# A four-layer transformer program on one core: the third layer with its routing inside the scan stage, and the first layer's row additions five in four heads

## The chip, the cores and the metric

One core of a Trainium2 chip runs the whole program in one launch. The metric is the device time of that launch in microseconds, on the core; lower is better. TensorE multiplies (its weight loads run beside its multiplications), VectorE, ScalarE and GpSimd compute on rows of 128 partitions, and SyncE issues most transfers. In the profile they are PE (and PEld), DVE, ACT, POOL and SP.

## What is computed

A tensor of 4 x 512 tokens of width 128 goes through four layers; each is an attention or state-space block beside a mixture of experts, both added to the running sum x. The stages that the change touches:

- Layer 0, attention: 16 heads of width 8 over each of four sequences, plain softmax. Its mixture of 64 experts has been computed before; each expert's 32 rows have yet to be added to their tokens' rows.
- Layer 2, both halves. From the normalized input xn (router weights, then two of eight experts each):

```python
logits = xf.astype(jnp.float32) @ w_router.T
gates = jax.nn.softmax(logits, axis=-1)
topk_gates, topk_idx = jax.lax.top_k(gates, TOP_K)
...
expert_mask = expert_mask * (position_in_expert < capacity)
...
hidden = jax.nn.silu(xf @ w_gate.T)
for e in range(N_EXPERTS):
    y = y + combine[:, e:e + 1] * (hidden @ w_down[e].T)
```

and beside it a selective state-space block: two projections with silu (xi and res), a step size delta = log(1 + exp(...)) clipped to 1e-5..0.1, an input term, an output term, and for each of 16 states the recurrence h[t] = exp(delta a)[t] h[t-1] + u[t] along the 512 tokens. The 16 states are summed, multiplied with the output term and res, and projected out.

## The kernel before

The program is a row of stages; each is a block of its own with one instruction stream per engine, and a stage ends on all engines before the next begins. Order on an engine is the order in which the code writes the instructions; between engines there are semaphores.

**Layer 0's heads** (`small_heads`, tag a0). 64 heads (4 sequences of 16) run through a pipeline, one step per head. In a step TensorE makes the scores twice (once to find each row's maximum, once turned) and the values' product; VectorE finds the maxima (L600); GpSimd splits each maximum into three bf16 parts in four small instructions (L548 to L554), which TensorE then needs (L425) so that the exponentials on ScalarE get them. Behind its four instructions GpSimd issues indirect transfers, 64 in all (L568): each adds one expert's 32 rows to a table in DRAM. Two tables take turns, so that a transfer waits for the one before the last (`put`). From head 4 on there are two behind each head, so they end behind head 35.

**Layer 2** (before: three stages). `norm_and_logits` (n2) normalizes x, turns it and makes the router's logits. `capacity_gates` (g2) picks the best two of eight experts, counts the tokens before each, and makes `gate`, the 16 x 8 weights of each partition; nearly all on VectorE as a chain of small instructions, with two exponentials on ScalarE and 32 small matmuls. `scan_and_ffn` (s2) then loads 14 weight tiles, whose issues are the first thing in its SyncE stream (L1528); every engine waits for all 14 (`loaded`).

`scan_and_ffn` goes in slots (b, n), b from -1 to 3 and n from 0 to 15. In a slot with b >= 0 VectorE does one recurrence (L1844, named s_h), then one piece of the next sequence's preparation (`prepare`: the step size's polynomial at n = 1 to 9, the input term and a bound on the state at n = 11 to 15), then two expert terms (`weigh`, L1799: x += product x gate). The expert terms run 8 slots early: 8 of 64 lie in slots before the first recurrence, and slots 48 to 55 have none. At n = 3 it mixes the sum of the sequence before (L1816), and at n = 7 adds its output to x (L1824). The recurrences write four buffers (`HB`); TensorE adds each to a PSUM sum (L1611, s_sum), and the recurrence four slots on waits for that. GpSimd makes xd as soon as delta is there (L1692), and behind the mixing of the sequence before three products, cr, xp and dr (L1697 to L1702).

TensorE's stream has one ring of five PSUM banks, `m`, for everything but the sums: projections, the three products of xi (dt, bm, cm) for the next sequence, written together at n = 0, the turned bound (L1601) and the expert products, two banks per pair of fills (L1573), written with every fourth expert term. A bank is opened only when its last reader is through (`m_open`), in the order of the list `order`, and what stands behind it on TensorE waits too:

```python
if b >= 0 and n == 0 and b + 1 < B:
    order += [("dt", b + 1), ("bm", b + 1), ("cm", b + 1)]
```

`out_products` (L1585 to L1587), at n = 5, waits for the mixed sum before its first product and then does four tiles of three products each.

Of the kernel before, what the change touches and what calls it, by code (L numbers as in the profile page):

```python
# [14 lines left out]
P = 128  # L15
# [299 lines left out]
def small_heads(nc, k, tag, parts, w_out, out_bias, causal, yrows, yacc=None):  # L315
# [13 lines left out]
    with ExitStack() as ctx:  # L329
# [206 lines left out]
        def _(pool):  # L536
# [19 lines left out]
            if not causal:  # L556
                for b in range(B):
                    for h in range(H):
                        step(b, h, lambda i: i >= 0)
                        n = H * b + h - 4  # L560
                        if n == 0:
                            pool.wait_ge(yc_in, 16)
                        for a in range(2):
                            e = 2 * n + a
                            if 0 <= e < 4 * H:
                                if n:
                                    pool.wait_ge(put[a], 16 * n)
                                pool.indirect_dma_start(yacc[a], bass.IndirectOffsetOnAxis(  # L568
                                    ap=k.seat[:, 16 * (e % 4) + e // 4:16 * (e % 4) + e // 4 + 1], axis=0), yc[:, e, :], None,
                                    compute_op=ALU.add).then_inc(put[a], 16)  # L570
# [460 lines left out]
def capacity_gates(nc, k, tag, capacity):  # L1031

    M = NT
    with ExitStack() as ctx:
        ph = Phase(nc, ctx, tag)
        below = ph.sb("below", [P, M, 8])  # L1040
        first = ph.sb("first", [P, M, 8])
        second = ph.sb("second", [P, M, 8])
        left = ph.sb("left", [P, M, 8])
        m = ph.sb("m", [P, 2, M])
        e = ph.sb("e", [P, 2, M])
        where = ph.sb("where", [P, M])
        tot = ph.sb("tot", [P, M])
        chain, best_ready, exp_done, both_ready, counted = (
            ph.sem(s) for s in ("chain", "best_ready", "exp_done", "both_ready", "counted"))
        both = ph.sb("both", [P, NT, 8], BF16)  # L1050
        before = ph.sb("before", [P, NT, 8], BF16)
        ex = ph.sb("ex", [P, M, 8])
        ps = ph.banks("ps", 1)
        lg = k.logits[:, 0:M * 8].rearrange("p (m e) -> p m e", e=8)
        gate = k.gate[:, 0:M * 8].rearrange("p (m e) -> p m e", e=8)
        wide = [P, M, 8]
        iota8 = bc(k.iota[:, 0:8].unsqueeze(1), wide)
        block = ctx.enter_context(nc.Block())

        @block.vector  # L1060
# [1778 lines left out]
```

## Time and profile before

| what | us |
|---|---|
| median of 3 runs | 2207.71 |
| lowest, highest | 2204.81, 2207.71 |
| the profiled execution | 2203.68 |
| its span, first to last instruction | 2201.9 |
| PE busy | 1924.9 (87%) |
| DVE busy | 1522.3 (69%) |
| ACT busy | 979.7 (44%) |
| POOL busy | 562.9 (26%) |
| mean granted TensorE clock | 0.94 |

The span is a row of stages that hide nothing of each other, so a share of the whole says little of one of them. Layer 0's heads lie from about 99 to 372 us, layer 2 from 820 to 1070 us, and layer 3 fills the rest. The page's first part has the busy times; a clock of 1.00 means 2.4 GHz, and 0.50 means 1.2 GHz.

### The profile page before, as it was taken

How to read it: one execution, taken by the hardware profiler on the slowest of the kernel's cores; microseconds unless marked ns; L12 is line 12 of the kernel's file. 1: busy time of each engine (PE TensorE's matmuls, PEld its weight loads, DVE VectorE, ACT ScalarE, POOL GpSimd, SP SyncE). 2: the span in 40 equal slices, each digit the busy share in tenths (PEclk: the TensorE clock that was granted, in tenths of full speed). 3: DMA queues.
4: the chain of work that ended last, by engine and by line, in shares of the span. 5: the costliest groups of instructions: out<-in, count | busy, mean ns of one | idle time of the engine just before them, and what ended most of it. 6: DMA issues, size and time to landing. Idle time of an engine off the chain costs nothing. (4 is left out here: it accounts for less than half of the span.)

```text
span 2201.9 us, 31669 instructions
## 1 busy us (share of the span) xinstructions
PE 1924.9 (87%) x9697; PEld 1011.3 (46%) x9697; DVE 1522.3 (69%) x4803; ACT 979.7 (44%) x2286; POOL 562.9 (26%) x967
## 2 busy tenths in 40 slices
PE   5588898449999965888699999999999999999998
PEld 3222333326655533333444444444444444466666
DVE  6566775627677663778688878877887777865554
ACT  3266665214376643422143333333333333267776
POOL 3478621340044410112000000000000000077777
PEclk9689999669999986999899999999999999999999
DMA  8432220663021200000144344442222111434332
GB/s 295 120 45 30 28 61 1 265 158 64 22 42 41 41 6 28 1 0 0 46 106 97 96 106 119 109 100 81 63 71 64 58 58 51 132 118 136 122 117 86
DMA packets 140765, 175.13 MB, mean 80 GB/s; under 512 B 15236, under 2 KB 117802, under 8 KB 139960
## 3 DMA queue, kind: packets, MB, share of 16 engines
q1 hardware_dynamic: 130328, 149.37, 23.8%
q0 software_dynamic: 10272, 23.73, 5.0%
q8 instruction: 82, 1.34, 0.2%
q14 instruction: 83, 0.68, 0.1%
HBM read 118.58 MB, written 54.48 MB: 79 GB/s over the span
## 5 line engine op out<-in xcount | busy, mean ns | idle before, releaser
L2514 DVE SCALAR_TENSOR_TENSOR x<-f_m,f_gs,x 128x128 f32<-128x128 f32 x1024 | 349.8, 345 | 86.1 <-PE f_m L2347 81.0
L600 DVE TENSOR_REDUCE a_nmax<-a_s 128x1 f32<-128x512 f32 (+3 forms) x512 | 278.9, 585 | 138.8 <-PE a_s L414 81.2
L2514 DVE SCALAR_TENSOR_TENSOR f_val<-f_m,gate,f_val 128x128 f32<-128x128 f32 x896 | 305.8, 344 | 68.2 <-PE f_m L2347 63.2
L2100 POOL TENSOR_SCALAR a_lg<-a_lg,a_rinv 128x256 f32<-128x256 f32 (+1 forms) x256 | 210.8, 843 | 482.2 <-DVE a_rinv L2137 481.8
L2347 PE MATMUL f_m<-f_wv,xnT 128*128 128x512 f32 x512 | 262.6, 597 | 4.6 <-DVE f_val L2514 4.6
L2347 PE MATMUL f_m<-f_wo,f_oT 128*128 128x512 f32 x512 | 261.5, 595 | 2.2 <-DVE f_val L2514 1.1
L519 ACT ACTIVATE a_pT<-a_st 128x512 f32<-128x512 f32 (+3 forms) x512 | 228.6, 520 | 31.2 <-PE a_st L440 14.0
L414 PE MATMUL a_s<-t_kp,t_qp 96*128 96x512 bf16 (+3 forms) x512 | 166.7, 361 | 4.9 <-DVEq L584 4.3
L437 PE MATMUL a_st<-t_qp,t_kp 99*128 99x512 bf16 (+3 forms) x512 | 162.9, 353 | 1.7 <-ACT a_pT L519 1.7
L2347 PEld LDWEIGHTS f_m<-f_wo,f_oT 128*128 128x128 f32 x512 | 95.5, 190 | 127.1 <-issue 107.3
L526 ACT CAST t_qp<-a_m 3x512 bf16<-3x512 f32 x128 | 73.9, 577 | 137.0 <-PE a_m L425 136.8
L2355 PE MATMUL f_s<-xnT,f_qT 128*128 128x512 f32 x256 | 134.6, 607 | 0.0
L2063 ACT ACTIVATE a_lg<-a_lg,a_nmax 128x256 f32<-128x256 f32 (+1 forms) x256 | 120.9, 476 | 29.4 <-DVE a_nmax L2130 29.4
L452 PE MATMUL a_o<-a_pT,t_vp 128*32 128x512 f32 (+3 forms) x1024 | 115.9, 527 | 15.9 <-ACT a_pT L519 10.4
L2347 PEld LDWEIGHTS f_m<-f_wv,xnT 128*128 128x128 f32 x512 | 90.3, 192 | 85.4 <-issue 70.2
L2436 ACT ACTIVATE f_val<-f_m,gate 128x128 f32<-128x128 f32 x128 | 46.9, 367 | 183.2 <-PE f_m L2347 179.5
L2457 ACT COPY f_pT<-f_t 128x512 f32<-128x512 f32 x128 | 74.9, 585 | 119.4 <-PE f_t L2363 119.1
L2130 DVE CUSTOM_DVE_ANT_0 a_lg<-a_m,a_rel 128x256 f32<-128x256 f32 (+1 forms) x256 | 85.0, 387 | 60.4 <-issue 60.4
L2307 POOL DMA_DIRECT2D band<-f_hole x16 | 18.6, 1160 | 390.3 <-PE f_m L2347 390.3
L2373 PE MATMUL f_o<-f_pT,f_val 128*128 128x512 f32 x256 | 115.2, 592 | 0.0
L1844 DVE TENSOR_TENSOR_SCAN s_h<-s_da,s_u 128x512 f32<-128x512 f32 x64 | 82.4, 1295 | 24.5 <-PE s_sum L1611 24.1
L2363 PEld LDWEIGHTS f_t<-ident,f_prob 128*128 128x128 f32 x512 | 63.8, 141 | 70.2 <-issue 65.9
(397 smaller groups left out, 3461.1 us busy)
## 6 DMA issues: line engine op xcount, KB each, us to landing
a_rel<-band SPq DMA_DIRECT2D x64, 512.0 KB, 4.5
band<-f_hole POOLq DMA_DIRECT2D x16, 1032.0 KB, 9.7
f_wv<-f_wv_in SPq DMA_DIRECT2D x32, 512.0 KB
f_wo<-f_wo_in SPq DMA_DIRECT2D x32, 512.0 KB, 3.5
band<-f_rows SPq DMA_DIRECT2D x64, 256.0 KB, 3.7
w_gate_up<-f_wgu_in SPq DMA_DIRECT2D x4, 1536.0 KB, 19.1
t_qp<-parts SPq DMA_DIRECT2D x192, 32.0 KB
t_kp<-parts SPq DMA_DIRECT2D x192, 32.0 KB
```

The lines of the kernel that those rows point to most:

```text
L414: last = pe.matmul(ps[:, 0:n], qp[0:MR, h, qt * P:(qt + 1) * P], kp[0:MR, h, 0:n], start=True, stop=not causal)
L437: last = pe.matmul(out[:, q0:T], kp[0:KT, i % H, kt * P:(kt + 1) * P], qp[0:KT, i % H, q0:T], start=True, stop=not causal)
L452: last = pe.matmul(o_ps[32 * j:32 * j + 32, q0:T], vp[:, g % 4, kt, j, :], pT[:, g % 2, j, kt, q0:T], start=(kt == 0), stop=(kt == QT - 1) ...
L519: act.activation(pT[:, g % 2, i % 4, kt, q0:T], st_ps[w % R][:, q0:T], ACT.Exp).then_inc(exp_done, 1)
L600: v.tensor_reduce(nmax[:, h % 4, qt:qt + 1], s_ps[(b * H * QT + u) % R][:, 0:n], AX.X, ALU.max, negate=True)\
L2063: last = act.activation(lg[:, g % 2, half, p, c0:c0 + w], lg[:, g % 2, half, p, c0:c0 + w], ACT.Exp, bias=nmax[:, g % 2, p, qt:qt + 1], sc ...
L2100: last = pool.tensor_scalar(lg[:, g % 2, half, p, c0:c0 + n], lg[:, g % 2, half, p, c0:c0 + n], rinv[:, g % 2, p, qt:qt + 1], None, ALU.mult)
L2130: last = v.tensor_tensor_reduce(lg[:, g % 2, half, p, c0:c0 + w], ps[:, c0:c0 + w], rel[:, h % 4, qt, 2 * P - w:2 * P], 1.0, 3.0e38, ALU.a ...
L2347: pe.matmul(ps[:, :], left, w[:, g % 2, i % 2, :], start=True, stop=True).then_inc(full, 1)
L2355: pe.matmul(s_ps[u % 2][:, :], qT[:, g % 2, qt * P:(qt + 1) * P], tokens(g), start=True, stop=True).then_inc(s_done, 1)
L2373: last = pe.matmul(o_ps[:, :], val[:, g % 3, kt, :], pT[:, g % 2, kt, :], start=(kt == 0), stop=(kt == QT - 1))
L2514: ins = v.scalar_tensor_tensor(out, ps[:, e * P:(e + 1) * P], gate, out, ALU.mult, ALU.add)
```

## The change

In layer 0 the additions begin one head earlier, behind head 3, and are spread: transfer number e goes behind the head where n x 5 // 4 passes e, so that one, one, one and two stand behind four heads. They end behind head 54.

In layer 2 the second and third stage become one. The 14 loads are issued in the stage before, behind the router's weights, and the largest (wd) has a semaphore of its own that only the expert products wait for. The routing chain stands in VectorE's stream at the head of `scan_and_ffn`, with pieces of sequence 0's preparation between its links, and its counting matmuls in TensorE's stream behind all projections, into the bank of the output products. The ring `m` has four banks and holds projections and expert products alone; dt, bm, cm and the turned bound share one bank `x`, each waiting for the reader of the last (`turn`). They stand at n = 0, 2, 5 and 14. z has two buffers, and dt of sequence 1 is made ahead. The expert terms are no longer early: term j is weighed in slot j. The output products stand at n = 6, with the bias as one product 512 wide and the four of dr ahead of the wait for the mixed sum; their addition to x stands at n = 10 in place of 7.

```diff
-                        n = H * b + h - 4
+                        n = H * b + h - 3
...
-                        for a in range(2):
-                            e = 2 * n + a
-                            if 0 <= e < 4 * H:
-                                if n:
-                                    pool.wait_ge(put[a], 16 * n)
+                        for e in range(max(n, 0) * 5 // 4, min(max(n + 1, 0) * 5 // 4, 4 * H)):
+                            if e >= 2:
+                                pool.wait_ge(put[e % 2], 16 * (e // 2))
...
-    S, E, NB, HB = 16, 8, 5, 4
+    S, E, NB, HB = 16, 8, 4, 4
...
+    FIRST = [("xi", 0), ("res", 0), ("hid", 0, 0), ("hid", 0, 1), ("xi", 1)]
+    REST = [("res", 1), ("hid", 1, 0), ("hid", 1, 1)]
+    REST += [f for b in range(2, B) for f in (("xi", b), ("res", b), ("hid", b, 0), ("hid", b, 1))]
+    ring = FIRST + REST + [f for p in range(B * PAIRS_Y) for f in fills_of(p)]
+    aside = [("dt", 0), ("dt", 1), ("bm", 0), ("cm", 0), ("peak", 0)]
+    for b in range(1, B):
+        aside += [("dt", b)] * (b > 1) + [("bm", b), ("cm", b), ("peak", b)]
...
-        @block.sync
-        def _(sp):
-            for dst, src in loads:
-                sp.dma_start(dst, src).then_inc(loaded, 16)
...
+            def project_aside(name):
+                kind, b = name
+                m_read(("xi", b))
...
+                if turn[name]:
+                    pe.wait_ge(x_free, turn[name])
...
+                pe.matmul(x_ps[:, :], left, xi[:, b, :], start=True, stop=True).then_inc(x_full, 1)
...
             def out_products(b):
-                pe.wait_ge(mixed, b + 1)
-                pe.wait_ge(dr_ready, b + 1)
...
+                pe.matmul(o_ps[:, :], k.ones[0:1, :], b_o[:, :, :].rearrange("a i d -> a (i d)"), start=True, stop=False,
+                          skip_group_check=True)
+                pe.wait_ge(dr_ready, b + 1)
...
+                pe.wait_ge(mixed, b + 1)
...
+            for name in FIRST:
                 project(name)
+            for name in aside[0:4]:
+                project_aside(name)
+            for name in REST:
+                project(name)
+            count()
+            pe.wait_ge(k.wd_in, 16)
+            experts(0)
+            turn_peak(0)
...
+                    if b + 1 < B:
+                        if n == 0 and b:
+                            project_aside(("dt", b + 1))
+                        if n == 2:
+                            project_aside(("bm", b + 1))
+                        if n == 5:
+                            project_aside(("cm", b + 1))
+                        if n == 14:
+                            turn_peak(b + 1)
+                    if t % 4 == 0 and t // 4 + 1 < B * PAIRS_Y:
+                        experts(t // 4 + 1)
...
+            act.activation(nought[:, :], a_slow[:, :], ACT.Exp).then_inc(table, 1)
+            act.wait_ge(table, 3)
             decays(0)
...
+                    if b + 1 < B:
+                        prepare_slot(b + 1, n)
+                    weigh(t)
+                    if b >= 1 and n == 3:
+                        mix(b - 1)
+                    if b >= 1 and n == 10:
+                        add_out(b - 1)
...
+            norm_and_logits(nc, k, "n2", d["f2_wr"], 8, early=early)
+            scan_and_ffn(nc, k, "s2", N * 5 // 32)
```

GpSimd in layer 0's heads, before, for one head (yacc is the table in DRAM, a_nmax the maxima):

```order
L548 TENSOR_TENSOR a_m<-a_nmax,a_zero 128x4
L550 TENSOR_TENSOR a_mrest<-a_nmax,a_m 128x4
L552 TENSOR_TENSOR a_m<-a_mrest,a_zero 128x4
L554 TENSOR_TENSOR a_m<-a_mrest,a_m 128x4
L568 DMA yacc<-a_yc,seat 2080x128 x2
```

The same with the change, behind heads 5, 6 and 7:

```order
L566 DMA yacc<-a_yc,seat 2080x128
L548 TENSOR_TENSOR a_m<-a_nmax,a_zero 128x4
L550 TENSOR_TENSOR a_mrest<-a_nmax,a_m 128x4
L552 TENSOR_TENSOR a_m<-a_mrest,a_zero 128x4
L554 TENSOR_TENSOR a_m<-a_mrest,a_m 128x4
L566 DMA yacc<-a_yc,seat 2080x128 x2
L548 TENSOR_TENSOR a_m<-a_nmax,a_zero 128x4
L550 TENSOR_TENSOR a_mrest<-a_nmax,a_m 128x4
L552 TENSOR_TENSOR a_m<-a_mrest,a_zero 128x4
L554 TENSOR_TENSOR a_m<-a_mrest,a_m 128x4
L566 DMA yacc<-a_yc,seat 2080x128
```

Two transfers stand behind every fourth head alone, and one behind each of the other three.

TensorE in layer 2, before, from the end of one sequence through slot 5 of the next (s_wd: expert products, s_w_fold and s_w_x: dt, bm, cm; s_h: adding a recurrence):

```order
L1615 MATMUL s_sum<-s_corr,ident 128x512
L1565 MATMUL s_m<-s_xi,s_w_fold 128x512
L1565 MATMUL s_m<-s_xi,s_w_x 128x512 x2
L1573 MATMUL s_m<-s_wd,s_hid 128x512 x4
L1611 MATMUL s_sum<-s_h,ident 128x512 x4
L1573 MATMUL s_m<-s_wd,s_hid 128x512 x4
L1611 MATMUL s_sum<-s_h,ident 128x512 x2
L1585 MATMUL s_o<-s_w_o,s_dr 128x128
L1586 MATMUL s_o<-s_b_o,ones 128x128
L1587 MATMUL s_o<-s_w_o,s_y 128x128
```

With the change, the same stretch through slot 6:

```order
L1451 MATMUL s_x<-s_xi,s_w_fold 128x512
L1473 MATMUL s_m<-s_wd,s_hid 128x512 x4
L1525 MATMUL s_sum<-s_h,ident 128x512 x2
L1451 MATMUL s_x<-s_xi,s_w_x 128x512
L1525 MATMUL s_sum<-s_h,ident 128x512 x2
L1473 MATMUL s_m<-s_wd,s_hid 128x512 x4
L1525 MATMUL s_sum<-s_h,ident 128x512
L1451 MATMUL s_x<-s_xi,s_w_x 128x512
L1525 MATMUL s_sum<-s_h,ident 128x512 x2
L1483 MATMUL s_o<-s_b_o,ones 128x512
L1487 MATMUL s_o<-s_w_o,s_dr 128x128 x4
L1491 MATMUL s_o<-s_w_o,s_y 128x128 x4
```

bm and cm moved from ahead of the first sum to slots 2 and 5 and into the bank x, and the output products moved one slot back, in three groups.

## Rows read from the trace of the kernel before

**Rows 1.** Timeline of POOL, layer 0's heads: start, us, line, [idle before <-releaser]

```profile
117.71 0.49 POOL L548 TENSOR_TENSOR a_m<-a_nmax,a_zero 128x4 bf16<-128x4 f32 x1
...
138.88 0.66 POOL L548 TENSOR_TENSOR a_m<-a_nmax,a_zero 128x4 bf16<-128x4 f32 x1
...
143.06 0.67 POOL L548 TENSOR_TENSOR a_m<-a_nmax,a_zero 128x4 bf16<-128x4 f32 x1
...
256.37 0.66 POOL L548 TENSOR_TENSOR a_m<-a_nmax,a_zero 128x4 bf16<-128x4 f32 x1
...
261.79 0.21 POOL L548 TENSOR_TENSOR a_m<-a_nmax,a_zero 128x4 bf16<-128x4 f32 x1 [1.63 <-DVE a_nmax L600]
...
265.54 0.20 POOL L548 TENSOR_TENSOR a_m<-a_nmax,a_zero 128x4 bf16<-128x4 f32 x1 [2.70 <-DVE a_nmax L600]
...
298.20 0.20 POOL L548 TENSOR_TENSOR a_m<-a_nmax,a_zero 128x4 bf16<-128x4 f32 x1 [2.16 <-DVE a_nmax L600]
...
360.30 0.58 POOL L548 TENSOR_TENSOR a_m<-a_nmax,a_zero 128x4 bf16<-128x4 f32 x1 [2.16 <-DVE a_nmax L600]
```

**Rows 2.** Stretches: PE, PEld, DVE, ACT, POOL busy us, PEclk, DMA share, GB/s

```profile
838.70:851.00 12.30, 1.01 (x32) 0.93 (x32) 9.60 (x42) 1.67 (x3) 0.00 (x0) 0.50 0.00 1
851.00:862.00 11.00, 0.00 (x0) 0.00 (x0) 0.00 (x0) 0.00 (x0) 0.99 (x2) 0.50 0.47 140
...
939.80:987.40 47.60, 39.42 (x98) 17.64 (x97) 36.77 (x66) 12.41 (x20) 5.80 (x5) 0.93 0.00 1
```

**Rows 3.** Timelines of PE, ACT and DVE, from the loads to the first recurrence

```profile
862.08 0.79 PE L1533 MATMUL s_sum<-s_w_dt,s_w_dl 16*128 16x128 f32 x2 [13.46 <-DMA s_wd<-f_wd_in]
...
877.55 1.88 PE L1565 MATMUL s_m<-xnT,s_wg 128*128 128x512 f32 x4
...
887.11 1.28 ACT L1658 ACT_TABLE_LOAD   x1 [3.61 <-DVE s_delta L1743]
888.40 0.72 ACT L1658 ACTIVATE s_da_slow<-s_delta,s_a_slow 128x512 f32<-128x512 f32 x1
...
870.16 0.75 DVE L1730 TENSOR_SCALAR s_z<-s_m,s_b_fold 128x512 f32<-128x512 f32 x1 [6.68 <-PE s_m L1565]
...
891.80 1.21 DVE L1755 TENSOR_TENSOR_SCAN s_s<-s_da_slow,s_s 128x512 f32<-128x512 f32 x1
893.05 0.69 DVE L1757 TENSOR_REDUCE s_peak<-s_s 128x1 f32<-128x512 f32 x1
...
896.10 1.22 DVE L1844 TENSOR_TENSOR_SCAN s_h<-s_da,s_u 128x512 f32<-128x512 f32 x1 [0.45 <-ACT s_da L1662]
```

**Rows 4.** Waits, layer 2: us in total, times, longest

```profile
DVE s_h L1844 <- PE s_sum L1611: 24.1, 6, 7.8
```

**Rows 5.** Timeline of DVE, the recurrences, and POOL's products beside them

```profile
939.81 1.22 DVE L1844 TENSOR_TENSOR_SCAN s_h<-s_da,s_u 128x512 f32<-128x512 f32 x1 [0.43 <-PE s_sum L1611]
...
967.98 0.69 DVE L1824 TENSOR_TENSOR x<-s_o,x 128x512 f32<-128x512 f32 x1 [2.85 <-PE s_o L1587]
...
987.37 1.22 DVE L1844 TENSOR_TENSOR_SCAN s_h<-s_da,s_u 128x512 f32<-128x512 f32 x1 [0.42 <-PE s_sum L1611]
...
1035.04 4.57 DVE L1844 TENSOR_TENSOR_SCAN s_h<-s_da,s_u 128x512 f32<-128x512 f32 x4 [0.41 <-PE s_sum L1611]
...
1040.11 7.15 DVE L1844 TENSOR_TENSOR_SCAN s_h<-s_da,s_u 128x512 f32<-128x512 f32 x4
1048.90 0.69 DVE L1824 TENSOR_TENSOR x<-s_o,x 128x512 f32<-128x512 f32 x1 [1.64 <-PE s_o L1587]
...
1062.07 0.59 DVE L1799 SCALAR_TENSOR_TENSOR x<-s_m,gate,x 128x128 f32<-128x128 f32 x2
...
1069.50 0.69 DVE L1824 TENSOR_TENSOR x<-s_o,x 128x512 f32<-128x512 f32 x1 [4.58 <-PE s_o L1587]
```

**Rows 6.** The timeline of POOL there, in sequence 1

```profile
948.77 1.26 POOL L1697 TENSOR_TENSOR s_cr<-s_cm,s_res 128x512 f32<-128x512 f32 x1 [22.55 <-DVE s_y L1816]
950.01 1.56 POOL L1698 TENSOR_SCALAR s_xp<-s_xi,s_dpar 128x512 f32<-128x512 f32 x1
```

More of the change, by code:

```diff
@@ L1477, in scan_and_ffn @@
+        first, second, left, below, ex, gate = (ph.sb(s, [P, NT, E]) for s in (
+            "first", "second", "left", "below", "ex", "gate"))
+        best, weight, where, tot = ph.sb("best", [P, 2, NT]), ph.sb("weight", [P, 2, NT]), ph.sb("where", [P, NT]), ph.sb("tot", [P, NT])
+        both, before = ph.sb("both", [P, NT, E], BF16), ph.sb("before", [P, NT, E], BF16)
+        w_fold = ph.sb("w_fold", [P, P])
         b_fold = ph.sb("b_fold", [P, 1])
-        dpar = ph.sb("dpar", [P, 1])
-        a_log = ph.sb("a_log", [P, S])
@@ L1786, in _ @@
             latest = {}
+            links = [0]
             def weigh(j):
@@ new lines, in _ @@
+            choose(left[:, :, :], 1, second)
+            link_up(v.tensor_tensor(weight[:, 1, :], best[:, 1, :], best[:, 0, :], ALU.subtract))
+            v.sem_inc(shares_ready, 1)
+            size_input(0)
+            size_input(1)
+            v.tensor_tensor(both[:, :, :], first[:, :, :], second[:, :, :], ALU.add).then_inc(both_ready, 1)
+            v.wait_ge(a_exp, 1)
+            v.tensor_scalar(a[:, :], a[:, :], -1.0, -5.0, ALU.mult, ALU.max).then_inc(a_raw, 1)
+            log_terms(0, 2)
@@ new lines, in _ @@
+            v.wait_ge(a_raw, 2)
+            v.tensor_scalar(a[:, :], a[:, :], -0.01, None, ALU.min).then_inc(a_raw, 1)
+            log_terms(0, 3)
+            v.wait_ge(a_raw, 3)
+            v.tensor_reduce(a_slow[:, :], a[:, :], AX.X, ALU.max).then_inc(a_raw, 1)
+            log_terms(0, 4)
+            v.wait_ge(both_ready, 1)
+            total = v.tensor_copy(before[:, 0, :], both[:, 0, :])
+            for i in range(1, NT - 1):
+                chain(total)
+                if i <= 4:
+                    log_terms(0, 4 + i)
+                if i == 5:
+                    step_size(0)
+                settle()
+                total = v.tensor_tensor(before[:, i, :], before[:, i - 1, :], both[:, i, :], ALU.add)
@@ new lines, in _ @@
+            state_input(0, 13)
+            link_up(v.tensor_tensor(gate[:, :, :], first[:, :, :], second[:, :, :], ALU.add))
+            v.wait_ge(counted, 1)
+            v.tensor_scalar(left[:, :, :], o_ps[:, 0:NT * E].rearrange("p (m e) -> p m e", e=E), float(capacity), None,
+                            ALU.is_lt).then_inc(routed, 1)
+            v.wait_ge(routed, 1)
+            link_up(v.tensor_tensor(gate[:, :, :], gate[:, :, :], left[:, :, :], ALU.mult))
+            state_input(0, 15)
```

419 lines of the change are left out of this document (172 added, 247 removed).

## The prediction

> **What bounds the kernel now.** I read the page first, for the row of stages, then the two changed stages by themselves: the table of waits to see which engine keeps which, and the timeline of the engine that is kept, for the price of each wait.
>
> *Layer 0's heads.* GpSimd's timeline gives the pace, since its first small instruction (L548) comes once per head. Behind a head with two transfers the next L548 comes 4.18 us later, 138.88 to 143.06, with no idle time before it: GpSimd is the bound [rows 1]. Heads 5 to 36 take 256.37 - 117.71 = 138.66 us, 4.47 each. Once the transfers are over GpSimd sits waiting for VectorE's maxima (1.63 and 2.70 us before two of its heads), and heads 47 to 63 take 360.30 - 298.20 = 62.10 us for 16, 3.88 each [rows 1]. That is the stage's pace without transfers.
>
> *Layer 2* is a chain on VectorE with four kinds of waiting. First 12.3 us of routing in which TensorE is busy for 1.01 us, at half clock, then 11.0 us of loads in which nothing but two fills on GpSimd runs [rows 2]. Then 34.0 us from TensorE's first product (862.08) to the first recurrence (896.10), in which projections, step size and bound wait for each other [rows 3]. In the recurrences VectorE waits 24.1 us for the sums on TensorE, six times [rows 4]; three of the six are the 0.4 us at a sequence's start [rows 5], which leaves 24.1 - 1.3 = 22.8, or 7.6 for each of sequences 0, 1 and 2. The code names the cause: cm, in the five-bank ring, needs a bank that VectorE empties only with a later expert term, and the sums stand behind it on TensorE. Last, the output products: 2.85 us of waiting in sequences 1 and 2, 1.64 in sequence 3 and 4.58 at the end [rows 5].
>
> **The change, part by part.** All sums are made against the profiled execution, 2203.68 us, whose span is 2201.9; it stands 4.0 below the median of the runs.
>
> *A. Additions five in four heads.* Two transfers take 4.18 less GpSimd's own four instructions of 0.2 and their gaps (about 1.1), so about 1.6 each. A head that is free of them leaves GpSimd the 1.63 us or more of idle time shown, so a single transfer is hidden by the wait for VectorE; were that wait gone, it would cost its 1.6. A double one makes a head of at least 4.18; the head it follows (h = 2 of each four) is 265.54 - 261.79 = 3.75 long without [rows 1]. Bounds: 0 where the pipeline takes the 0.43 up in its next wait, 13 x 0.43 = 5.6 where not; half of it, 2.8, since TensorE waits for GpSimd's split in some heads and for others in the rest. The gain is 31 x (4.47 - 3.88) = 18.3, less 2.8: **15.5 us**, between 12.7 and 18.3. The last transfer moves from head 35 to 54, still nine heads ahead of the reading of the tables.
>
> *B. Up to the first recurrence*, from the routing's start at 838.7: before 57.4 us. After, step by step, mostly with the distances of rows 3. TensorE may begin at once, since the loads are issued in the stage before and the 11.0 of rows 2 are gone. Its first product to the first z took 8.1 us (862.08 to 870.16); one more projection stands ahead now, 0.86 (four matmul records, two products, in 1.88, overlapping by a little): 9.0. VectorE's routing up to the second maximum (13 links of about 0.32, with the fold before it: 5.7) is hidden there. Then the shared bank passes from hand to hand, z of sequence 0 and 1, bm, cm, four readers of 0.7 and three products of about 0.9: 5.5. Eleven more projections at 0.86, 9.5, and the last silu 0.8. The step size, the counting and GpSimd's products lie under these; without that cover they would be some 9 us. Then a table load and a short exponential 1.5, the slow decay 0.8, the bounding recurrence and its maximum 2.0 (1.21 and 0.69), three gate operations 1.0, the flag 0.5, four more gate operations 1.1, the flag's loading and first recurrence 0.5. Sum 32.2; gain **25.2 us**. What is late next is the last projections' silu, no longer delta. Ends: 21 (each hand-over 1 us dearer) and 29 (TensorE at full clock from the start: four early products at 0.86 and not 1.88).
>
> *C. The 64 slots*, first recurrence to last expert term: before 1062.66 - 896.10 = 166.6, in pieces 43.7, 47.6, 47.7 and 27.6 [rows 3, 5]. Sequence 0 loses 7.6 and z's 0.75: 35.3. Sequences 1 and 2 lose 7.6 and 2.85 each: 37.2. Sequence 3 loses 1.64 and takes the eight unweighed slots' terms, 8 x 0.5: 30.0. New cost: GpSimd's three products behind the mixing (1.26, 1.56 and again 1.26 [rows 6]) ran in sequences 1 and 2 while VectorE stood still, and now run under recurrences. What that costs a row shows: in sequence 3, where they did, four recurrences took 7.15 in place of 4.57 [rows 5]. So 2.6 more for sequences 1 and 2 each; it is already in sequence 3. Sum 35.3 + 39.8 + 39.8 + 30.0 = 144.9; gain **21.7 us**. TensorE needs 36 products of 0.86 and 3.8 for output and bound in sequence 1, 34.8, under VectorE's 39.8; in sequence 3, 28.4 under 30.0.
>
> Here a page speaks against the change. By the Trainium skill (SBUF - State Buffer, section "Who interferes with whom") a VectorE instruction with two SBUF inputs and a GpSimd instruction that reads SBUF exclude each other for the whole instruction. By that rule the three products would cost their full 4.1 us per sequence and the sum would be 3 us worse over sequences 1 and 2; the 2.6 of rows 5 says that a part of them falls beside instructions that read PSUM.
>
> *D. The end.* From the last recurrence's end TensorE needs 2.0 for sum and correction. Bias and dr's products (2.2) now lie beside the mixing, and 1.5 remain behind them, in place of mixing (0.8) and the 4.58 of waiting [rows 5]: **1.6 us**.
>
> Sum: 15.5 + 25.2 + 21.7 + 1.6 = 64.0, so 2203.7 - 64.0 = 2139.7 for an execution like the profiled one, and 2143.7 for one like the median. I predict 2142.
>
> **The rivals.**
> 1. *The transfers bound layer 0 still.* A transfer's landing, not its issue, could be what GpSimd waits for, and double heads could cost more than 0.43. For it: it now waits at 52 heads, not 32. Against: two of a table are now mostly 1.6 heads apart, over 6 us. Gain 5 in place of 15.5: 2152.
> 2. *TensorE sets the pace of the slots.* For it: 39.42 us busy in 47.6 of sequence 1 and a clock of 0.93 [rows 2], by which 34.8 becomes 37.4; with products now in six places of a sequence, waits no longer overlap. Sequences 1 to 3 would cost some 4 more each: 2154.
> 3. *Full exclusion of GpSimd and VectorE*, as a mechanism of this kernel: cr, xp and dr each hold up a recurrence for their whole length, 4.1 a sequence in place of 2.6, and xd and the small chain in B likewise: 4.5 more, 2146. That is the page's rule above; the 7.15 of rows 5 shows it in part only.
> 4. *Slower: the four-bank ring.* A pair of expert banks can be filled only when VectorE is through with the pair before the last, and the fill, four products of 0.86, stands ahead of the sum on TensorE. If each of the 15 fills is exposed with the sum behind it, 4.3 each, 64.5 us come back and the time is 2207 or more; with a hand-over of 0.4 at each, 2213. It decides from where a fill and a sum take longer than the four slots that the recurrence buffers give. Those are 4 x 2.3 = 9.2 us in sequences 0 to 2, and 4 x 1.7 = 6.8 in sequence 3, so it would need fills twice as long.
> 5. *The change doesn't do what it says*: the loads are not early, because issues on SyncE wait for the router's stage. 11 us come back: 2153. Nothing stands before them in that stream but one load.
>
> **How the numbers follow.** Forecast 0.62 (2131 to 2152, from the ends of A and B and half of the contention), rival 1 0.10, rival 2 0.12, rival 3 0.10, rival 4 0.02, rival 5 0.02; 0.02 stays for what no row shows. Ends worked out: best 2142 - 2.8 - 3.8 - 5 (no contention in sequences 1 and 2) = 2130; worst without a rival 2142 + 2.8 + 4.2 + 3 = 2152. The range takes in rivals 1 to 3 with some of the forecast's spread: 2130 to 2161. A measurement of this kernel tells about 0.2%, 4.4 us, from no change. Faster by more than that: all but rival 4 and half of the remainder, 0.97; within 0.2%: 0.01; slower: 0.02.
>
> **What would show it.** In the profile after: L548 every 3.9 us on average over heads 5 to 54, with idle time before nearly all; layer 2 some 48 us shorter, with no stretch of loads between logits and first product; the first recurrence some 32 us behind the logits; no wait of VectorE for sums over 1 us; recurrences beside GpSimd's products in sequences 1 and 2 over 1.3 us. The prediction is wrong if VectorE waits on TensorE's sums or expert products in every fourth slot, if head pairs with two transfers are over 4.6 us, or if the routing chain, not the projections, is what the first recurrence waits for.

## The result and the profile after

The median fell from 2206.33 us (2204.81 to 2207.71, four runs) to **2136.8 us** (2135.41 to 2138.83, four runs): a ratio of 0.9686, with a 95% interval of 0.9669 to 0.9703, or 69.5 us. The profiled execution took 2137.22 us with a span of 2135.4, 66.5 us under the one before.

Where the 66.5 came from, by the start of a stage's first instruction in either timeline (us):

| Stretch | Before | After | Gained | Predicted |
|---|---|---|---|---|
| start to head 0 of layer 0 | 102.00 | 101.34 | 0.7 | 0 |
| heads 5 to 63 (A) | 242.59 | 223.16 | 19.4 | 15.5 |
| head 63 to the norm of layer 2 | 459.98 | 459.82 | 0.2 | 0 |
| logits to the first recurrence (B) | 57.4 | 32.8 | 24.6 | 25.2 |
| the 64 slots (C) | 166.6 | 142.7 | 23.9 | 21.7 |
| last expert term to the end of the outputs (D) | 7.5 | 5.3 | 2.2 | 1.6 |
| norm of layer 3 to the end | 1130.4 | 1134.9 | -4.5 | 0 |

The last row is the one that nobody forecast: unchanged code that took longer. The experiments come to it.

**Layer 0.** GpSimd's timeline over four heads (start, duration, then what it waited for; each head begins with its first L548), against [rows 1]:

```profile
135.52 0.21 POOL L548 TENSOR_TENSOR a_m<-a_nmax,a_zero 128x4 bf16<-128x4 f32 x1 [0.49 <-DVE a_nmax L598]
...
136.71 1.33 POOL L566 DMA_INDIRECT yacc<-a_yc,seat  x1
138.34 1.33 POOL L566 DMA_INDIRECT yacc<-a_yc,seat  x1 [0.30 <-issue]
139.27 0.65 POOL L548 TENSOR_TENSOR a_m<-a_nmax,a_zero 128x4 bf16<-128x4 f32 x1
...
141.42 1.33 POOL L566 DMA_INDIRECT yacc<-a_yc,seat  x1 [0.67 <-DMA yacc<-a_yc,seat]
142.78 0.21 POOL L548 TENSOR_TENSOR a_m<-a_nmax,a_zero 128x4 bf16<-128x4 f32 x1
...
147.56 0.21 POOL L548 TENSOR_TENSOR a_m<-a_nmax,a_zero 128x4 bf16<-128x4 f32 x1 [2.25 <-DVE a_nmax L598]
...
150.23 0.20 POOL L548 TENSOR_TENSOR a_m<-a_nmax,a_zero 128x4 bf16<-128x4 f32 x1 [0.16 <-DVE a_nmax L598]
```

The head with two transfers takes 3.75 us (135.52 to 139.27) and the four heads from there, to 150.23, take 14.71. The waits of GpSimd in this stage (us in total, times, longest) say the same: it now waits mostly for VectorE.

```profile
POOL a_m L548 <- DVE a_nmax L598: 39.9, 34, 3.1
POOL yacc L566 <- DMA yacc<-a_yc,seat: 5.6, 9, 1.1
```

**Up to the first recurrence**, the timelines of TensorE, ScalarE and VectorE, against [rows 3]:

```profile
818.45 0.76 PE L1423 MATMUL s_sum<-s_w_dt,s_w_dl 16*128 16x128 f32 x2 [0.77 <-PEq L61]
...
828.42 1.10 PE L1451 MATMUL s_x<-s_xi,s_w_fold 128*128 128x512 f32 x2 [1.01 <-DVE s_z L1656]
830.53 1.10 PE L1451 MATMUL s_x<-s_xi,s_w_x 128*128 128x512 f32 x2 [1.01 <-DVE s_z L1656]
832.50 1.10 PE L1451 MATMUL s_x<-s_xi,s_w_x 128*128 128x512 f32 x2 [0.87 <-ACT s_bm L1554]
833.43 1.02 PE L1441 MATMUL s_m<-xnT,s_w_in 128*128 128x512 f32 x2
...
843.08 0.60 ACT L1548 ACTIVATE s_hid<-s_m 128x512 f32<-128x512 f32 x1 [0.26 <-PE s_m L1441]
843.69 1.28 ACT L1587 ACT_TABLE_LOAD   x1
```

No loads stand between the logits and the first product. The last projection's silu ends at 843.68, the recurrence follows at 851.27. The shared bank goes from hand to hand with a gap of 0.9 to 1.0 us on TensorE each time.

**The slots.** Stretches (length, busy us of PE, PEld, DVE, ACT, POOL, then PEclk, DMA share, GB/s), one for each sequence, against [rows 2], and VectorE's waits in them, against [rows 4]:

```profile
851.30:886.00 34.70, 28.43 (x63) 10.75 (x62) 34.63 (x62) 16.33 (x27) 1.27 (x1) 1.00 0.00 1
886.00:925.00 39.00, 34.88 (x91) 15.15 (x90) 38.35 (x65) 12.53 (x20) 7.03 (x5) 1.00 0.00 0
925.00:964.00 39.00, 37.63 (x92) 17.47 (x91) 38.03 (x64) 12.53 (x20) 7.61 (x5) 0.91 0.00 1
964.00:996.00 32.00, 30.98 (x82) 13.45 (x82) 29.61 (x54) 0.00 (x0) 5.77 (x3) 1.00 0.00 1
```

```profile
DVE s_h L1833 <- PE s_sum L1525: 2.0, 3, 0.8
```

VectorE is busy 34.63 of 34.70 us in sequence 0 and 38 of 39 in the next two: it is the bound, and 24.1 us of waiting have become 2.0. GpSimd's products now run beside its work, against [rows 5, 6]:

```profile
895.67 2.05 POOL L1612 TENSOR_TENSOR s_cr<-s_cm,s_res 128x512 f32<-128x512 f32 x1 [22.79 <-DVE s_y L1759]
897.70 2.00 POOL L1613 TENSOR_SCALAR s_xp<-s_xi,s_dpar 128x512 f32<-128x512 f32 x1
899.78 1.26 POOL L1617 TENSOR_TENSOR s_dr<-s_xp,s_res 128x512 f32<-128x512 f32 x1
...
896.58 1.70 DVE L1671 SCALAR_TENSOR_TENSOR s_lp<-s_lp,s_z 128x512 f32<-128x512 f32 x1
898.19 0.59 DVE L1743 SCALAR_TENSOR_TENSOR x<-s_m,s_gate,x 128x128 f32<-128x128 f32 x2
898.71 1.21 DVE L1833 TENSOR_TENSOR_SCAN s_h<-s_da,s_u 128x512 f32<-128x512 f32 x1
899.84 1.75 DVE L1671 SCALAR_TENSOR_TENSOR s_lp<-s_lp,s_z 128x512 f32<-128x512 f32 x1
...
903.17 0.66 DVE L1671 SCALAR_TENSOR_TENSOR s_lp<-s_lp,s_z 128x512 f32<-128x512 f32 x1
```

Two log terms take 1.70 and 1.75 where 0.66 is usual, and GpSimd's product 2.05 where [rows 6] has 1.26. The ends of the instructions show how: for cr, dr, recurrences and log terms the engines take turns, each until the other's instruction is nearly over. cr (s_cr) begins at 895.67 but ends only 1.06 us after the recurrence that began at 895.44 has ended (896.66); the log term of 896.58 ends 0.56 us after cr (897.72), and the one of 899.84 ends 0.55 us after dr (901.04). Two kinds of work are not held up: the expert terms between them, which read PSUM, keep their 0.59, and the recurrence of 898.71 keeps its 1.21 beside xp, which has one tensor as input (in the kernel before, a recurrence beside xp took 1.64, from 1043.39 us). Summed so, contention costs VectorE 2.1 us in sequence 1, 1.6 in 2 and 1.05 in 3.

### The profile page after: what moved, and what is told of

The parts are those of the page before. It is cut to its first block and busy times, and to the rows that moved or that the text cites. A ratio compares the mean times of both kernels' runs of the same rounds, so it can differ in the third digit from the quotient of the medians.

```text
span 2135.4 us, 31607 instructions
## 1 busy us (share of the span) xinstructions
PE 1912.6 (90%) x9672; PEld 1007.3 (47%) x9672; DVE 1525.5 (71%) x4802; ACT 979.4 (46%) x2286; POOL 563.6 (26%) x967
## 5 line engine op out<-in xcount | busy, mean ns | idle before, releaser
L2579 DVE TENSOR_REDUCE f_nmax<-f_s 128x1 f32<-128x512 f32 x128 | 87.2, 681 | 6.2 <-PE f_s L2342 6.2
```

The lines of the kernel that those rows point to most:

```text
L2579: v.tensor_reduce(nmax[:, u % 4:u % 4 + 1], s_ps[u % 2][:, :], AX.X, ALU.max, negate=True)\
```

## The experiments

They were run in three sessions, each with the kernel before beside it: 2208.66, 2204.80 and 2204.41 us. A ratio is against the kernel before of the same session; stretches are read from the profiled execution of each.

**Each half alone.** The diff of the first is the additions' hunk of the change and nothing else; the second is the changed kernel with that hunk undone.

> The kernel before, with only the additions of layer 0 spread five in four heads; the scan stage is the old one. Theory (the two halves of the change add, and double heads cost nothing): heads 5 to 63 shorten by 19.4 us as in the profile after, so about 2206.3 - 20 = 2186 us, ratio 0.991. Rival (the prediction's own term, double heads cost half of 0.43 each): 15.5 less, 2191. Rival (a shift of layer 0 is given back further on, at a clock that falls at another stage's start): 2190 to 2195 with heads 5 to 63 still 19.4 shorter. Layer 3 from its norm to the end tells the last apart: 1130.4 us in the profile before, 1134.9 after.

> The changed kernel with the two additions per head of before put back; the new scan stage alone. Theory (the halves add): layer 2 is 50.7 us shorter, so about 2206.3 - 50 = 2156 us, ratio 0.977. Rival (each half alone is worth more than its share of the sum, since the whole gave back 4.4 us in layer 3): 2152 with layer 3 at 1130.4. If layer 3 takes 1134.9 here and not with the additions alone, the 4.4 belongs to the scan stage's end; if in neither, to neither.

Measured: the additions alone 2192.19 us, ratio 0.9930 (0.9909 to 0.9952); the scan stage alone 2162.02, ratio 0.9795 (0.9773 to 0.9816). In their profiles heads 5 to 63 take 222.57 with the additions alone (20.0 gained) and layer 2, norm to norm, 202.85 with the scan alone (48.3 gained; 50.7 in the full change). But layer 3 took 1134.5 and 1134.9: the 4 us are lost in both, so they belong to neither half. The spans' gains are 15.5 and 44.9, 60.4 together, against 66.5; with layer 3's 4.1 lost once and not twice it is 64.5, and the 2.4 of the next paragraph make it 66.9. So stage by stage the halves add. By the ratios they come to 0.70% and 2.05%, some 61 us against 69; the difference of 8 is at the edge of what these intervals allow, and which stages hold it in the unprofiled runs is not shown.

The scan stage alone also began 2.4 us later than in the full change, in identical code. The stretches from TensorE's first hand-over on (columns as above) show the granted clock fall between its two levels, 2.4 and 1.2 GHz:

```profile
847.25:852.65 5.40, 3.52 (x5) 0.92 (x6) 4.08 (x12) 2.36 (x7) 0.00 (x0) 0.72 0.00 2
852.65:857.25 4.60, 4.60 (x8) 1.97 (x7) 4.29 (x11) 2.98 (x4) 1.47 (x2) 0.58 0.00 0
```

In the profile after, the clock was 1.00 there. Four of the other profiled kernels have the same spell: from TensorE's first product to the first recurrence the loads-late kernel, three more products, bm and cm at slot 0 and cm in the ring took 34.7 to 35.0 us, and the full change 32.8.

**Loads late.** The loads issued by SyncE in the scan stage again:

```
-            norm_and_logits(nc, k, "n2", d["f2_wr"], 8, early=early)
-            scan_and_ffn(nc, k, "s2", N * 5 // 32)
+            norm_and_logits(nc, k, "n2", d["f2_wr"], 8)
+            scan_and_ffn(nc, k, "s2", N * 5 // 32, early)
```

> The changed kernel with the 14 loads of the scan stage issued inside it again and not in the stage before. Theory: the 11.0 us in which before only loads ran come back whole, because the new order needs 13 of them before TensorE's first product and VectorE's routing: 2136.8 + 11 = 2148 (2146 to 2150). Rival (the routing of 5.7 us that was hidden under projections, or other work, covers a part, or the last load, which has a semaphore of its own and is the largest, no longer counts): 3 to 8 us come back, 2140 to 2145.

Measured: 2150.49 us, ratio 0.9739 (0.9713 to 0.9766). TensorE's first product waits for the last small load, on TensorE's timeline:

```profile
828.41 0.79 PE L1427 MATMUL s_sum<-s_w_dt,s_w_dl 16*128 16x128 f32 x2 [7.80 <-DMA s_b_o<-s_b_o_in]
```

That is 25.4 us behind the norm's start, not 18.4: 7.0 later, and the first recurrence 8.9. The other 1.9 lie behind the first product, in the half-clock spell just named, which four kernels with early loads have too. So the early loads are worth 7.0 in the profile, not the 11.0 of [rows 2]: TensorE now waits for the last small load and no longer for the largest. By the ratios it is 11.7, with an uncertainty of some 7. The ratio cannot tell 7 from 11, the trace can.

**Projections between the hand-overs.** res, hid, hid and xi of sequences 1 and 2 go into the gaps of the shared bank:

```
-            for name in aside[0:4]:
-                project_aside(name)
-            for name in REST:
+            for i in range(4):
+                project_aside(aside[i])
+                project(REST[i])
+            for name in REST[4:]:
                 project(name)
```

> The changed kernel, with the first four of the other sequences' projections put between dt, dt, bm and cm in TensorE's order. In the profile after TensorE stands idle about 1 us at each of the three hand-overs of the shared bank, at 828.42, 830.53 and 832.50. Theory (TensorE's projections are what the first recurrence waits for): three products of 0.86 go into the gaps, 2 to 3 us gained, 2134.3. Rival (the last silu is bound by ScalarE's own row of short instructions, or by the routing on VectorE): under 0.7 us gained, 2136.5. Rival (a hand-over is delayed, since each of its products may wait behind a projection): up to 1.5 us lost, 2138.

Measured: 2141.03 us, ratio 0.9702 (0.9678 to 0.9727); no gain. First product to first recurrence is 33.2 us, after 32.8. TensorE's timeline:

```profile
832.86 1.02 PE L1441 MATMUL s_m<-xnT,s_w_in 128*128 128x512 f32 x2
835.80 1.13 PE L1441 MATMUL s_m<-xnT,s_w_in 128*128 128x512 f32 x2 [1.92 <-ACT s_res L1549]
836.77 3.54 PE L1441 MATMUL s_m<-xnT,s_wg 128*128 128x512 f32 x4
```

The four were done in the gaps, but the ring was then full until ScalarE, behind a table load, emptied it: 1.92 us of waiting, and behind it two products at half clock (3.54 for 1.88). What was won in three small gaps was lost in one and behind it.

**No additions at all** (the transfers and their waits are taken out of GpSimd's stream).

> The changed kernel without the 64 additions of layer 0: what they add is left out, and the tables are read at a fixed head. Theory (one transfer in three heads and two in the fourth hide wholly in GpSimd's wait for VectorE): heads 5 to 63 take 223 us as in the profile after, within 1.5. Rival (the prediction's: a double head costs up to 0.43 us each, 13 of them): 217.5 to 220 us.

Measured: heads 5 to 63 take **223.23 us; with the 64 additions it was 223.16**. That the two agree to a tenth is in part luck: heads 5 to 10 took 15.7 to 19.9 us in the eleven profiles that have these additions, where the granted clock ranged from 0.73 to 1.00, and 18.5 at 0.79 in both of these. The steady part is what shows it. Heads 10 to 63 take 204.76 without additions and 204.70 with them (204.7 to 206.1 over the eleven), in the same row of distances, 3.75, 3.52, 4.77 and 2.68 us. GpSimd now waits 137.7 us for VectorE between 110 and 306 us, not 39.9. So transfers one or two to a head are free, and rival 1 is out. The whole took 2145.18 us, ratio 0.9718 (0.9699 to 0.9737), more than the changed kernel: 3.2 us of it lie ahead of head 0, in the same code, and 3.8 us between head 63 and the norm of layer 2, where the reading of the tables was moved too, and that was not followed up.

**Three more products on GpSimd** in each sequence:

```
+                for i in range(3):
+                    pool.tensor_tensor(spare[:, i, :], xi[:, b, :], res[:, b, :], ALU.mult)
```

> The changed kernel, with three more products of 1.3 us each on GpSimd behind dr in every sequence (their results are used by nothing). Theory (contention is partial, as in the profile after, where three products per sequence lengthened VectorE's instructions by 1.05 to 2.1 us): 1 to 2 us more in each of sequences 1 to 3, 3 to 6 in all. Rival (full exclusion): each holds VectorE for its 1.3, so 3.9 a sequence, 11.7 in all. Rival (what was seen has to do with VectorE's mixing and not with GpSimd): nothing.

Measured: 2148.62 us, ratio 0.9739 (0.9720 to 0.9759). Sequences 1, 2 and 3 are 2.7, 2.6 and 1.5 us longer, 6.9 for nine products, 0.76 each. Timelines of VectorE and of GpSimd:

```profile
906.34 1.76 DVE L1836 TENSOR_TENSOR_SCAN s_h<-s_da,s_u 128x512 f32<-128x512 f32 x1
908.03 1.68 DVE L1674 SCALAR_TENSOR_TENSOR s_lp<-s_lp,s_z 128x512 f32<-128x512 f32 x1
909.63 0.59 DVE L1746 SCALAR_TENSOR_TENSOR x<-s_m,s_gate,x 128x128 f32<-128x128 f32 x2
```

```profile
906.99 5.99 POOL L1620 TENSOR_TENSOR s_spare<-s_xi,s_res 128x512 f32<-128x512 f32 x3
```

A recurrence that meets a product is 0.5 us longer (1.76 for 1.21), a log term 1.0 (1.68 for 0.67), and the product itself takes 2.0 where one alone took 1.27. The delay is shared between both engines, since they take turns as in the profile after: the first of the three products ends 1.06 us after the recurrence of 906.34 (908.10), and the log term of 908.03 ends 0.55 us after that product (909.16). What a product costs VectorE on balance is less than its 1.27, because the expert terms run beside it. The sum lies just above the range given for partial contention, far under the 11.7 of the rival; that rival priced the turns too high, and the turns themselves are there.

**bm and cm at slot 0, in their own bank.**

```
-                        if n == 2:
+                        if n == 0:
                             project_aside(("bm", b + 1))
-                        if n == 5:
                             project_aside(("cm", b + 1))
```

> The changed kernel, with bm and cm of the next sequence at slot 0 on TensorE, where the kernel before has them, still in a bank of their own. Theory (the 7.6 us waits of before came from the shared ring, not from the place in the order): the four recurrence buffers give 9.2 us and TensorE is held 5.5 at most, so sequences 0 to 2 change by less than 0.8 us each. Rival (the place is what counts): 3 to 8 us in sequences 1 and 2, less in sequence 0, 6 to 16 in all.

Measured: 2154.61 us, ratio 0.9763 (0.9744 to 0.9782), and **my theory fell**: sequences 0, 1 and 2 are 5.9, 3.0 and 2.7 us longer, by waits for sums of 5.8, 5.0 and 3.6. The timelines of TensorE (first fence) and ScalarE name what I had overlooked:

```profile
863.11 2.05 PE L1451 MATMUL s_x<-s_xi,s_w_x 128*128 128x512 f32 x2 [6.03 <-ACT s_bm L1553]
864.95 5.39 PE L1473 MATMUL s_m<-s_wd,s_hid 128*128 128x512 f32 x8
...
902.70 2.04 PE L1451 MATMUL s_x<-s_xi,s_w_x 128*128 128x512 f32 x2 [2.05 <-DVE s_z L1655]
905.68 2.04 PE L1451 MATMUL s_x<-s_xi,s_w_x 128*128 128x512 f32 x2 [0.93 <-ACT s_bm L1553]
```

```profile
856.79 5.61 ACT L1571 ACTIVATE s_da<-s_delta,s_a 128x512 f32<-128x512 f32 x9
862.30 0.67 ACT L1553 ACTIVATE s_bm<-s_x,s_b_bc 128x512 f32<-128x512 f32 x1
```

The bank that dt, bm and cm share makes each wait for the reader of the last. In sequence 0 that is ScalarE, which copies bm only after the last of this sequence's decays: 6.03 us. In sequence 1 it is VectorE, which reads dt's product late (2.05 us), and then bm's copy (0.93 us); sequence 2 is alike. After the idle time TensorE works at half clock (2.05 for a product of 1.02, 5.39 for a fill of 3.60), with the sums behind it.

**cm in the ring, at slot 0**; bm stays in its own bank at slot 2. The ring gets `("cm", b + 1)` ahead of the second pair of each sequence, ScalarE and GpSimd wait for it there, and TensorE takes it at slot 0.

> The changed kernel, with cm of sequences 1 to 3 put back into the ring of expert banks, at slot 0 as before. Theory (the ring is the cause: the fill behind cm gets a bank that VectorE empties only at slot 3, and the next one waits until cm is copied, behind the mixing): VectorE waits 2 to 8 us for a sum near slot 4 of sequences 0, 1 and 2, 6 to 24 us in all. Rival (a bank of its own was not needed): under 1 us per sequence.

Measured: 2153.37 us, ratio 0.9755 (0.9736 to 0.9774). Waits of 4.4, 3.9 and 4.9 at slot 4; the sequences are 4.5, 2.1 and 3.4 us longer. Here TensorE's fill waits for VectorE, and in the kernel before cm itself did (second fence, its timeline of TensorE in sequence 0):

```profile
868.27 3.57 PE L1477 MATMUL s_m<-s_wd,s_hid 128*128 128x512 f32 x4 [7.74 <-DVE x L1758]
```

```profile
904.20 2.04 PE L1565 MATMUL s_m<-s_xi,s_w_x 128*128 128x512 f32 x2 [5.12 <-DVE x L1799]
906.04 5.07 PE L1573 MATMUL s_m<-s_wd,s_hid 128*128 128x512 f32 x8
```

So the ring is a cause, and 10.1 us come back with cm alone in it. The 11.6 us of bm and cm at slot 0 have another cause: it comes with the shared bank, which the kernel before did not have. In that kernel bm had a bank of the ring and its copy began at 900.16, 4 us before cm could start; cm waited for VectorE alone. Neither a bank of their own at slot 0 nor the later slot with cm in the ring is enough; the change needs the bank and the slots. The last two rows show the half clock in the kernel before as well (2.04 for 1.02, 5.07 for 3.60): 2.5 us of its wait in sequence 0.

**Layer 3's 4 us.** In the stretches of 4 us from TensorE's first product of the attention (columns as above), one of before, then three of after:

```profile
1913.39:1917.39 4.00, 3.23 (x18) 1.96 (x20) 1.10 (x5) 0.58 (x1) 0.00 (x0) 1.00 0.01 2
```

```profile
1842.84:1846.84 4.00, 3.75 (x4) 1.15 (x4) 0.75 (x1) 0.21 (x1) 0.00 (x0) 0.50 0.01 2
1846.84:1850.84 4.00, 3.48 (x17) 2.62 (x18) 1.31 (x12) 1.52 (x6) 0.00 (x0) 0.50 0.00 0
1850.84:1854.84 4.00, 4.00 (x8) 1.78 (x9) 2.72 (x11) 3.26 (x13) 0.00 (x0) 0.84 0.54 147
```

TensorE is idle some 3 us between the stages, and then finds the clock at either level. The attention took 288.5 us in the full-clock case and 292.5 to 292.7 in the other. Three kernels tested whether filling idle stretches with products that nothing reads holds the clock up: three products at the end of the stage ahead of the attention; five at the start of every norm; and both, with the interleaving of projections from above and two more products in its 1.92 us gap. The first two edits:

```
+            for i in range(3):
+                pe.matmul(s_ps[0][:, :], k.ident[:, :], k.xnT[:, 0:T], start=True, stop=True)
```

```
+            for i in range(5):
+                pe.matmul(lps[-1][:, :], k.ident[:, :], k.x[:, 0:4, :].rearrange("p t d -> p (t d)"), start=True, stop=True)
```

> The changed kernel, with three products on TensorE that nothing uses in the idle 3.3 us before layer 3's attention. In ten profiled runs so far this attention took 288.5 us in two (granted clock 1.00 in its first 8 us), 290.2 in one and 292.6 in seven (clock 0.50). Theory (the clock falls because TensorE stands idle there, and whether it does is chance, not the change): with the gap filled the clock stays at 1.00, the attention takes 288.5 us, and the median falls by 3 to 4 us against the changed kernel run beside it. Rival (the fall has to do with something else, for instance the many short expert products before it): 292.6 as before, no gain, or 0.3 lost since the hand-over comes later.

> The changed kernel, with five products on TensorE that nothing uses at the start of each of the four norm stages, where TensorE is idle for 6 us and more and then works at a granted clock of 0.50 (800.03 to 824 in the profile after). Theory (the same as for the hand-over): the clock is at 1.00 when the transposes begin; TensorE's 10.4 us of work in each norm halve where VectorE and ScalarE let it, and the scan stage starts at full clock: 2 to 4 us per norm, 8 to 16 in all. Rival (transposes and logits wait for VectorE and ScalarE, not for TensorE): under 1 us per norm. Rival (no rise: what is added is at half clock as well): nothing, or up to 1.7 us lost per norm where the fifth product holds up the first transpose.

> The changed kernel with both fills, the interleaved projections, and two unused products in the 1.9 us in which TensorE waited behind them for ScalarE. Theory: the parts add; from the norm of layer 2 to the first recurrence 51.2 us become 46 (3 from the norm, 2.2 from the projections, which gave nothing alone because the clock fell in the 1.9 us gap), layer 3's attention takes 288.5; in all 12 to 20 us under the changed kernel. Rival (the first recurrence waits for ScalarE's silus, 16 of 0.6 to 0.7 with three table loads, whatever TensorE does): the projections' part is under 1 us.

> The changed kernel itself, for comparison on the same chip: 2136.8 us on the chip of the first measurement, 2137 to 2143 expected here. Theory (a shift of up to 4.1 us in layer 3, 2.3 before the first recurrence and others like them at stages' starts comes and goes with the clock from run to run): its profile differs from the first one in these places and nowhere by over 0.5 us in the 64 slots or in heads 5 to 63.

| Kernel | Median (us) | Ratio (95%) | Attention | Norm of layer 2 to first recurrence |
|---|---|---|---|---|
| changed, again | 2135.18 | 0.9686 (0.9667 to 0.9705) | 292.5 | 51.1 |
| hand-over filled | 2133.46 | 0.9676 (0.9660 to 0.9693) | 288.5 | 50.9 |
| norms filled | 2126.04 | 0.9645 (0.9623 to 0.9667) | 288.5 | 50.3 |
| all fills | 2126.13 | 0.9636 (0.9613 to 0.9659) | 288.5 | 48.3 |

*Hand-over.* TensorE's timeline with the fill:

```profile
1842.64 2.74 PE L2402 MATMUL f_s<-xnT,ident 128*128 128x512 f32 x6
1846.07 1.10 PE L1951 MATMUL a_m<-xnT,a_wq 128*128 128x512 f32 x2 [0.70 <-PEq L2211]
```

The gap is 0.70 and the clock stays full, 288.5 us, in both kernels that have the fill. Without it, of the twelve other profiled executions three had full clock (before, three more products, norms filled), one rose early (290.2) and eight were at 292.5 or more. Two of two against three of twelve points to the fill, but is no proof, and 1.7 us in the median is within the intervals. What is shown is that the 4.1 us are the clock's and not the change's: the same loss with either half of the change and none with three products more. How often the kernel before has full clock there is not known, since it has one profile. By the Trainium skill (TensorE: Matmul & The Clock Gate, section "What's actually happening") the throttled clock is the default, activity lifts it, and the moment depends on the phase at which the work begins, so that the same kernel measures differently from run to run; the runs here agree.

*Norms.* Of after and of the filled kernel, the idle stretch of layer 2's norm and that of its transposes and logits:

```profile
800.00:807.20 7.20, 0.00 (x0) 0.00 (x0) 6.50 (x44) 1.50 (x2) 0.00 (x0) 0.50 0.29 69
807.20:817.70 10.50, 10.40 (x48) 9.79 (x48) 3.86 (x16) 2.34 (x4) 0.00 (x0) 0.50 0.30 101
```

```profile
788.80:796.00 7.20, 6.03 (x10) 2.45 (x10) 6.52 (x44) 1.48 (x2) 0.00 (x0) 0.79 0.28 69
796.00:806.50 10.50, 9.69 (x48) 8.79 (x48) 3.86 (x16) 2.61 (x5) 0.01 (x1) 0.63 0.30 101
```

The clock rises under the added products and falls again to 0.63 in the narrow ones, although TensorE is busy 9.69 of 10.50 us. This norm gained 0.7 us, with all fills 2.4 (16.0 us to the first product in place of 18.4). Against the changed kernel beside it, the filled one gained 3.1 us up to head 0, 1.5 in the heads, 4.5 from there to layer 2's norm, lost 0.6 in layer 2 and gained 5.1 in layer 3, 4.0 of them in the attention, ahead of which this kernel fills nothing, so that they may be the chance described above. These make 13.6 us between the two profiled executions; the medians say 9.1: **with *all fills* the fastest version here**, 78 us under before. *All fills* add nothing that can be told from it. From first product to first recurrence they take 32.3 us, after 32.8, although the clock is 1.00 from 820 us on, 10 us behind the first product: as the rival had it, the projections' part is under 1 us. The ring is full behind cm's product until ScalarE has loaded its table and done the first silu, and TensorE's last seven products, 0.86 each, follow only then.

*The control* differs from the first profile by under 0.1 us in every sequence of slots; heads 5 to 63 took 221.9, 1.2 less than then, which is more than I had allowed; the difference lies in heads 5 to 10 (17.2 us at full clock, 18.5 at 0.79).

## Why the prediction was right or wrong

The time was 5.2 us under the forecast of 2142 and within its range. Against the sum of 64.0 the profiled executions differ by 66.5 and the medians by 69.5; two terms were too cautious, and an unforeseen loss, which came to the profiled execution by chance of the clock, set off a part of them. That the whole came so near is luck to that extent.

- **A was too small (15.5, measured 19.4).** The mis-sized term is "half of the 0.43 of a double head", 2.8: it measured nothing, as heads 10 to 63 without additions show. GpSimd's 4.18 was compared with one head of 3.75, while the pipeline evens out over four (14.71 for four heads). The rest is the pace. 3.88, taken from heads 47 to 63, is not that of heads 5 to 36, which ran at 3.78 (138.66 to 117.23 us for 31). The reason shows in the distances: four heads take 14.7 us, but once in 16, from the second sequence on (heads 26 to 30, 42 to 46, 58 to 62), they take 18.5 (4.55, 3.52, 4.77, 5.63). Heads 5 to 36 hold one such group, heads 36 to 63 two. Heads 36 to 63 in turn took 105.9, not 103.9: when the transfers of the kernel before ended, GpSimd was behind and did one head in 2.74 where 4.77 is usual. That gain of 2.0 us is gone with the change. Nor was 4.18 a head the whole of the old cost: one head took 7.87, with a wait of 3.99 for an addition to land.
- **B was right in sum (25.2, measured 24.6).** z came at +9.1 (9.0 forecast), the eleven projections took 9.45 (9.5), the hand-overs 5.9 (5.5). Of the gain the early loads carry 7.0 and not 11.0, so other terms carry more than was put down to them; which, no run tells apart.
- **C was a little small (21.7, measured 23.9).** Pieces of 35.2, 39.8, 39.2 and 28.4 against 35.3, 39.8, 39.8 and 30.0. The mis-sized term is the contention, 2.6 per sequence from [rows 5]: it is 2.1, 1.6 and 1.05. Its reading of that 2.6 was wrong as well: it took a part of the products to fall beside instructions that read PSUM, but the four recurrences of [rows 5] have no expert terms between them. The 2.6 is not 4.1 because the recurrence beside xp was only 0.43 us longer (1.64 for 1.21); those held up by cr and dr were 1.0 and 1.1 longer. After the change expert terms stand between them too. TensorE did come close, busy 30.98 of 32 us in sequence 3, and in three of the experiments' profiles VectorE waited 1.2 to 1.3 us for a sum at slot 60, each time with a granted clock of 0.7 to 0.9 about the sequence's start, where the profile after has 1.00.
- **The cause given for the 7.6 us waits holds, with a part left out.** The ring did hold cm back, as the 5.12 us row of the kernel before shows for sequence 0 (5.64 and 5.63 us in sequences 1 and 2), and cm in the ring brings 10.1 of the 22.8 us back. How the other 12.7 divide was not measured: that kernel has bm at slot 2 and four banks. Left out was the half clock behind TensorE's idle time. Not foreseen either was that the shared bank works only at the later slots. The change has both, but the prediction gave no reason for the slots, so that part of the gain was luck.
- **D** gave 2.2 against 1.6.
- **Rivals.** 1 (transfers) is out by the kernel without additions. 2 (TensorE) and 4 (the four-bank ring): no wait for a sum over 0.8 us in the profile after. 3 (full exclusion) is out by its price: 2.1, 1.6 and 1.05 us a sequence and not 4.1, and 0.76 per added product. The turns that it speaks of are there in the rows of cr and dr, but xp does not hold up a recurrence in the profile after, and expert terms run beside all three. 5 (loads not early) did not occur; it would have cost 7.0 and not 11.
- **Not in the prediction:** the clock at the start of a stage. The profiled execution before had full clock in layer 3's attention, and most profiles of the other kernels had not. So the profiled reference was 4 us fast there against the profile after, and 4.5 us of the gains elsewhere do not show in the difference of the two profiles. Its whole was 2203.68 us beside a median of 2206.33; that the 2.7 between them is this clock is likely, but not shown.

## What to carry to other kernels

Work that an engine does while it would wait anyway costs nothing until the idle time of several steps is used up: add the slack over the period of the pattern, not step by step. Where a change gives instructions a resource of their own, ask who must read it between two uses, and when: the shared bank ended one wait and would have made another at the old place. And before a few microseconds are put down to a change, compare the granted clock at the start of each unchanged stage.

## What was not expected of the hardware

- Half-clock spells at the start of stages come and go between executions of the same code: 4.1 us in layer 3's attention, 2.4 before the first recurrence, 1.4 in sequence 3. Whether they make the spread between runs is not shown, since no kernel but the changed one has a second profile.
- TensorE can be busy 92% of a stretch and still be granted 0.63 of its clock, in transposes and products of 8 columns.
- A product on GpSimd beside VectorE: 2.0 us for 1.27; on VectorE 0.5 us more for a recurrence of 1.21 and 1.0 more for a log term of 0.67, and nothing for operations with one input in PSUM. The Trainium skill (SBUF — State Buffer, section "Who interferes with whom") has the same pairs contend and gives the shared ports to whichever begins first, for the whole instruction. The expert terms' 0.59 agrees with it, and so do the ends of cr, dr and the log terms beside them; the recurrence of 1.21 us beside xp does not. The price on balance, 0.76 us per product, is below a product's length.
